# A graph network on one Trainium2 core: adjacency for 38 destination tiles, the other 11 tiles' first sums from gathered rows

## The chip, the cores and the metric

The kernel runs on one core of a Trainium2 chip. The metric is the time of one execution on the device in microseconds; lower is better. A profiled execution gives the trace from which all rows below are read. Engines: TensorE (PE, its weight loads PEld), VectorE (DVE), ScalarE (ACT), GpSimd (POOL), SyncE (SP, which only issues DMAs here). Each runs its own instructions in order and waits on semaphores for the others.

## What is computed

6250 nodes with 128 features, 100,000 directed edges sorted by destination. Four layers follow, each on the layer-normed, rectified state and added to it. The change touches only the first sum of layer 0 and what is made for it:

```python
h = jnp.maximum(_layernorm(x, axis=-1), 0.0)
# layer 0
msgs = x[src]
agg_sum = jax.ops.segment_sum(msgs, dst, num_segments=N)
cnt = jax.ops.segment_sum(jnp.ones((src.shape[0],)), dst, num_segments=N)
aggs = agg_sum / jnp.maximum(cnt, 1.0)[:, None]
out = jnp.concatenate([x, aggs], axis=1) @ W_fuse.T + b_fuse + alpha * x_spectral
# then batch norm, gelu; layer 1: relations, layer 2: attention and feed-forward
# layer 3: ten times
agg = jax.ops.segment_sum(norm[:, None] * xk[src], dst, num_segments=n)
xk = (1.0 - ALPHA) * agg + ALPHA * h
```

## The kernel before

**Tiles.** Nodes are cut into NT = 49 tiles of 128. Edges stand 128 to a column; column (or edge tile) k holds edges 128k and on, and since they are sorted it touches the destinations near 8k. `near(k)` lists its destination tiles, one or two of them; `near_last[m]` is the last column that touches tile m.

**The adjacency.** For each destination tile i the kernel builds the columns of a count matrix, source node by destination node, as fp8: BK = 26 blocks of BD = 5 destinations each. Keys of up to 128 edges of each block are gathered early by GpSimd (L881), decoded by VectorE (L2338 to L2345), counted (L2347) and turned by TensorE into `slot_c`, one column a block. All this holds NB blocks in BS columns of 128.

**The build loop** runs over i and over 13 pairs q of blocks. For a block VectorE writes two one-hots, of the source within its tile (L2365, 128 wide) and of source tile and destination (L2367, 245 wide), into a ring of HOT = 6. TensorE multiplies them (L1597). ScalarE copies a pair out of PSUM into `made`, a ring of MADE = 4 tiles (L1200). When a tile's 13 pairs are out, SyncE stores it to `adj` in DRAM (L688).

**Layer 0's sums** ride along: during tile i TensorE multiplies tile i-1's `made` by the node states y16, four of 49 products behind each pair (L1608, one behind the last). y16 holds the states as two f16 halves and a column of ones for the count. ScalarE copies the second half and the count out (L1190) at q = 3 of tile i+1, and VectorE adds both into C (L2356, L2357) before block k = 6 of it. Since the queues are in order, block 6 stands behind ScalarE's pairs 0 to 2.

**After the loop** the counts of captured edges are compared with the number of edges; the kernel takes its dense branch if all are there. **The last layer** already treats the tiles in two ways: for DENSE = 38 of them it loads `adj` again in each of ten steps; for the last POOLED = 11 it gathers the source rows of their edge tiles (L859), writes one-hots of the destinations on VectorE (L2277) and multiplies on TensorE (L1567). So the adjacency of tiles 38 to 48 is read by nothing but layer 0's sums.

## Time and profile before

| what | us |
|---|---|
| median of three runs | 5482.05 |
| the three runs | 5483.43, 5469.74, 5482.05 |
| profiled execution | 5473.77 |
| its span, first to last instruction | 5471.9 |

The page of the profile gives busy time by engine: TensorE 4486.4 us (82% of the span), VectorE 3022.5 (55%), ScalarE 1054.3, GpSimd 3214.8. These are means over stages with different limits. The stages: loads and preparation to 130 us, the build loop to 666, the rest of layer 0 to about 784, relations, attention, feed-forward, and from about 3040 the ten steps, in which TensorE is full. What the change is worth is read in the stage it touches.

### The profile page before, as it was taken

How to read it: one execution, taken by the hardware profiler on the slowest of the kernel's cores; microseconds unless marked ns; L12 is line 12 of the kernel's file. 1: busy time of each engine (PE TensorE's matmuls, PEld its weight loads, DVE VectorE, ACT ScalarE, POOL GpSimd, SP SyncE). 2: the span in 40 equal slices, each digit the busy share in tenths (PEclk: the TensorE clock that was granted, in tenths of full speed). 3: DMA queues.
4: the chain of work that ended last, by engine and by line, in shares of the span. 5: the costliest groups of instructions: out<-in, count | busy, mean ns of one | idle time of the engine just before them, and what ended most of it. 6: DMA issues, size and time to landing. Idle time of an engine off the chain costs nothing. (4 is left out here: it accounts for less than half of the span.)

```text
span 5471.9 us, 97167 instructions
## 1 busy us (share of the span) xinstructions
PE 4486.4 (82%) x33994; PEld 3739.4 (68%) x33994; DVE 3022.5 (55%) x9610; ACT 1054.3 (19%) x2965; POOL 3214.8 (59%) x3380
## 2 busy tenths in 40 slices
PE   1888849999999265566667799999999999999997
PEld 1555526666666265555555688888888888888886
DVE  5888845555555467777775543343434344343444
ACT  2888731111111201111115100000000000000000
POOL 1000027777776277777760567676767767676775
PEclk9999979999999567766778899999999999999999
DMA  3111122222222243434330566666666666665665
GB/s 121 75 75 72 76 64 67 66 67 66 67 67 57 63 97 97 94 96 98 95 85 36 159 193 187 189 196 184 199 188 194 187 185 201 185 197 184 196 190 181
DMA packets 353802, 696.74 MB, mean 127 GB/s; under 512 B 98849, under 2 KB 233287, under 8 KB 353024
## 3 DMA queue, kind: packets, MB, share of 16 engines
q1 hardware_dynamic: 245648, 466.34, 26.9%
q0 software_dynamic: 107648, 223.88, 16.0%
q8 instruction: 290, 4.75, 0.4%
q14 instruction: 216, 1.77, 0.1%
HBM read 596.34 MB, written 93.92 MB: 126 GB/s over the span
## 5 line engine op out<-in xcount | busy, mean ns | idle before, releaser
L809 POOL DMA_INDIRECT arena<-table,src_i x782 | 741.2, 948 | 904.7 <-DMA table<-A 666.6
L859 POOL DMA_INDIRECT arena<-table,src_i x890 | 846.0, 951 | 529.1 <-DMA table<-E 254.7
L859 POOL DMA_INDIRECT arena<-x_spill,src_i x890 | 847.2, 952 | 352.0 <-issue 252.4
L824 POOL DMA_INDIRECT E<-gat_table,src_i x782 | 755.6, 966 | 337.8 <-issue 234.4
L1364 PE MATMUL ps<-E,arena 128*128 128x288 f32 (+7 forms) x3116 | 790.8, 406 | 90.2 <-DMA arena<-table,src_i 88.1
L1549 PE MATMUL ps<-E,arena 128*128 128x256 f16 x6370 | 726.6, 275 | 58.8 <-DVEq L2268 46.4
L1549 PE MATMUL ps<-A,arena 128*128 128x256 f16 x6370 | 725.4, 275 | 0.6 <-issue 0.2
L1549 PEld LDWEIGHTS ps<-E,arena 128*128 128x128 fp8e4 x6370 | 627.6, 99 | 138.5 <-issue 60.8
L1364 PEld LDWEIGHTS ps<-E,arena 128*128 128x128 f32 x3116 | 507.6, 194 | 309.5 <-issue 145.1
L1549 PEld LDWEIGHTS ps<-A,arena 128*128 128x128 fp8e4 x6370 | 627.5, 99 | 78.9 <-issue 1.9
L2294 DVE SCALAR_TENSOR_TENSOR O<-ps,sc_b,O 128x128 f32<-128x128 f32 x260 | 91.2, 351 | 825.6 <-PE ps L1549 747.7
L1416 PE MATMUL ps<-arena,B 128*128 128x144 f32 x2332 | 530.8, 384 | 2.3 <-DVE arena L2026 2.3
L1929 DVE SCALAR_TENSOR_TENSOR E<-arena,pt 128x512 f32<-128x512 bf16 x782 | 527.5, 742 | 3.0 <-PE ps L1364 2.9
L1416 PEld LDWEIGHTS ps<-arena,B 128*128 128x128 f32 x2332 | 435.6, 257 | 2.5 <-issue 2.5
L1200 ACT ACTIVATE E<-ps 128x490 fp8e4<-128x490 f32 (+1 forms) x637 | 378.3, 595 | 101.6 <-PE ps L1597 84.9
L1427 PE MATMUL pt<-ident,E 128*128 128x128 f32 x56 | 26.0, 464 | 436.1 <-ACT E L1031 436.1
L1608 PE MATMUL pt<-arena,E 128*128 128x258 f16 x2401 | 371.8, 274 | 0.9 <-ACT E L1200 0.9
L2367 DVE TENSOR_SCALAR O<-arena 128x245 bf16<-128x245 bf16 x1274 | 365.8, 287 | 0.0
L1597 PE MATMUL ps<-O 128*128 128x245 bf16 x1274 | 279.1, 274 | 70.3 <-DVE O L2367 67.1
L1549 PE MATMUL pt<-E,arena 128*128 128x256 f16 x2940 | 330.8, 273 | 0.1
L1549 PE MATMUL pt<-A,arena 128*128 128x256 f16 x2940 | 330.7, 273 | 0.0
L2365 DVE TENSOR_SCALAR O<-arena 128x128 bf16<-128x128 bf16 x1274 | 320.4, 252 | 0.5 <-PE ps L1597 0.4
(325 smaller groups left out, 5549.5 us busy)
## 6 DMA issues: line engine op xcount, KB each, us to landing
arena<-adj SPq DMA_DIRECT2D x386, 784.0 KB
adj<-E SPq DMA_DIRECT2D x49, 784.0 KB, 3.3
arena<-table,src_i POOLq DMA_INDIRECT x1672
O<-dst_rows SPq DMA_DIRECT2D x112, 224.0 KB, 3.4
x_spill<-A SPq DMA_DIRECT2D x245, 64.0 KB
table<-E SPq DMA_DIRECT2D x245, 64.0 KB
arena<-x_spill,src_i POOLq DMA_INDIRECT x890
E<-gat_table,src_i POOLq DMA_INDIRECT x782, 3.3
```

The costliest lines, as they stand in the source:

```text
L809: pool.indirect_dma_start(out=rows_ring[:, k % RING, :], out_offset=None, in_=table, in_offset=bass.IndirectOffsetOnAxis(ap=src_i[:, k:k + ...
L824: pool.indirect_dma_start(out=att_rows[:, b % 3 * AB + at, :], out_offset=None, in_=gat_table, in_offset=bass.IndirectOffsetOnAxis(ap=src_ ...
L859: pool.indirect_dma_start(out=y_rows[:, g % ERING, k, :], out_offset=None, in_=(table, x_spill)[half], in_offset=bass.IndirectOffsetOnAxis ...
L1200: act.activation(made[:, i % MADE, :, 2 * BD * q:2 * BD * q + w], ps[pair % 4][:, 0:w * NT].rearrange("p (d j) -> p j d", j=NT), ACT.Copy, ...
L1364: mm = pe.matmul(ps[m % 4][:, (lo - WD * m) * BASES:(hi - WD * m) * BASES], rows_ring[:, k % RING, :], m_ring[:, k % MS, lo - first_dst(k) ...
L1416: mm = pe.matmul(ps[i % 2][:, 0:WL2], edge_hot[:, (2 * b + half) % 3, k % AH, i % 2 * P:(i % 2 + 1) * P], weighted_rows[:, b % 2, k, :], s ...
L1549: mm = pe.matmul(bank_of(x)[:, 0:2 * D], adj_ring[:, u, i * P:(i + 1) * P], y[:, i, :], start=(p == 0), stop=(p == NT - 1))
L1597: pe.matmul(ps[pair % 4][:, h * BW:(h + 1) * BW], hot_src[:, g % HOT, :], hot_code[:, g % HOT, 0:BW], start=True, stop=True).then_inc(sem( ...
L1608: mm = pe.matmul(pt[0][:, m % 2 * 512:m % 2 * 512 + 2 * LO], made[:, m % MADE, j, :], y16[:, j, :], start=(j == 0), stop=(j == NT - 1))
L1929: dve.scalar_tensor_tensor(m_ring[:, k % MS, :, :], bc(iota_h[:, 0:WD], BASES), dst_rel[:, k:k + 1], row_bc(made_c[:, c % 2, at, :], WD), ...
L2365: dve.tensor_scalar(hot_src[:, g % HOT, :], iota_h, slot_c[:, g // P, 0, g % P:g % P + 1], None, ALU.is_equal)
L2367: dve.tensor_scalar(hot_code[:, g % HOT, 0:BW], iota_w[:, 0:BW], slot_c[:, g // P, 1, g % P:g % P + 1], None, ALU.is_equal).then_inc(sem(" ...
```

## The change

The build loop, `adj`, `slot_c` and the keys go over DENSE = 38 tiles. For the other 11, layer 0's sums are made beside the loop:

- SyncE writes y16 to a new table `first_rows` (129 words a row) and the states to `table`, before the adjacency stores. `table` was written later and only in the other branch.
- GpSimd gathers 178 columns of source rows, in groups of EG0 = 16 into a ring of 32 rows that lies in A.
- VectorE writes a 256-wide f16 one-hot of the destination for each column (L2436 after the change), in groups of four, before block k = 16 of tiles 4 to 37.
- TensorE multiplies them (L1648) behind the last pair of tiles 4 to 37, about five columns a tile, 258 products in all.
- When a tile of the eleven is complete, ScalarE copies it out at q = 4 of the next tile and VectorE takes it over before k = 8. Ten are completed in tiles 8 to 36, the last in tile 37.
- The check of captured edges counts the edges of the eleven tiles too.

```diff
-NB = NT * BK
+NB = DENSE * BK
+EG0, HOT_BASE, USED_BASE = 16, 2, 3
...
+        first_rows = dram("first_rows", (NP, LO))
...
+        junk = E[:, 5120:5120 + ET]
+        dst_near = arena[:, 12096:12096 + ET - 600]
+        rows0 = A[:, 0:2 * EG0 * LO].rearrange("p (s f) -> p s f", f=LO)
+        hot0 = A[:, 2 * EG0 * LO:2 * EG0 * LO + EHOT * EG * P].bitcast(F16).rearrange("p (g k d) -> p g k d", g=EHOT, k=EG)
...
+        taken, edges_in, done0, done_in = 0, {}, [], {}
+        for i in range(DENSE + 1):
+            upto = max(0, min(EDGE_TILES, EDGE_TILES * (i - 3) // (DENSE - 4)))
+            edges_in[i] = range(taken, upto)
+            taken = max(taken, upto)
+            done0 += [i - 1] if i else []
+            done_in[i] = [m for x in edges_in[i] for m in range(DENSE, NT) if near_last[m] == edge_first + x]
+            done0 += done_in[i]
+        place0 = {m: p for p, m in enumerate(done0)}
+        hots_in = {i: [x // EG for x in edges_in[i] if x % EG == 0] for i in edges_in}
...
+            sp.wait_ge(sem("hT"), PTN)
+            sp.wait_ge(sem("y_lower"), PTN)
+            sp.dma_start(first_rows.rearrange("(t p) f -> p t f", p=P),
+                         arena[:, 0:NT * LO].rearrange("p (t f) -> p t f", f=LO)).then_inc(sem("table0"), 16)
+            sp.dma_start(table_v, nodes(A)).then_inc(sem("table0"), 16)
+
             adj_v = adj.rearrange("(j p) b -> p j b", p=P)
-            for i in range(NT):
+            for i in range(DENSE):
                 sp.wait_ge(sem("blocks_out"), (i + 1) * (BK // 2))
                 sp.dma_start(adj_v[:, i, 0:NP], made_u8[:, i % MADE, :]).then_inc(sem(f"adj_stored{i % MADE}"), 16)
             for k in range(MADE):
-                sp.wait_ge(sem(f"adj_stored{k}"), 16 * ((NT + MADE - 1 - k) // MADE))
+                sp.wait_ge(sem(f"adj_stored{k}"), 16 * ((DENSE + MADE - 1 - k) // MADE))
             sp.wait_ge(sem("judged"), 1)
             dense = sp.value_load(verdict[0:1, 0:1], min_val=0, max_val=1)
             with sp.If(dense == 1):
...
+            pool.wait_ge(sem("table0"), 32)
+            pool.wait_ge(sem("decoded"), 1)
+            for x in range(EDGE_TILES):
+                g = x // EG0
+                if g >= 2 and x % EG0 == 0:
+                    pool.wait_ge(sem("edge_used0"), USED_BASE + (g - 1) * (EG0 // EG))
+                pool.indirect_dma_start(
+                    out=rows0[:, x % (2 * EG0), :], out_offset=None, in_=first_rows,
+                    in_offset=bass.IndirectOffsetOnAxis(ap=src_i[:, edge_first + x:edge_first + x + 1], axis=0)
+                ).then_inc(sem(f"edge_rows{g % 2}"), 16)
             pool.wait_ge(sem("judged"), 1)
...
-            for i in range(NT + 1):
+            def sums_out(m):
+                p = place0[m]
+                act.wait_ge(sem("multiplied0"), p + 1)
+                if p >= 2:
+                    act.wait_ge(sem("agg0"), p - 1)
+                act.activation(lower_sum[:, p % 2, :], bank0_of(m)[:, D:2 * LO - 1], ACT.Copy).then_inc(sem("counted"), 1)
+
+            for i in range(DENSE + 1):
                 for q in range(BK // 2):
-                    if q == 3 and i >= 2 or i == NT and q == 6:
-                        m = i - 2 if q == 3 else i - 1
-                        act.wait_ge(sem("multiplied0"), m + 1)
-                        if m >= 2:
-                            act.wait_ge(sem("agg0"), m - 1)
-                        act.activation(lower_sum[:, m % 2, :], pt[0][:, m % 2 * 512 + D:m % 2 * 512 + 2 * LO - 1],
-                                       ACT.Copy).then_inc(sem("counted"), 1)
-                    if i == NT:
+                    if q == 3 and i >= 2:
+                        sums_out(i - 2)
+                    if q == 4 and i >= 1:
+                        for m in done_in[i - 1]:
+                            sums_out(m)
+                    if q == 6 and i == DENSE:
+                        sums_out(i - 1)
+                        for m in done_in[i]:
+                            sums_out(m)
+                    if i == DENSE:
...
-            for i in range(NT + 1):
+            def bank0_free(m):
+                if m >= 2 and m - 2 < DENSE and m < DENSE or m - 2 >= DENSE:
+                    pe.wait_ge(sem("agg0"), place0[m - 2] + 1)
+                    pe.wait_ge(sem("counted"), place0[m - 2] + 1)
+
+            def edge_products(x):
+                g, k, tile = x // EG, x % EG, edge_first + x
+                if x % EG0 == 0:
+                    r = x // EG0
+                    pe.wait_ge(sem(f"edge_rows{r % 2}"), 16 * BS + 16 * sum(
+                        min(EG0, EDGE_TILES - q * EG0) for q in range(r % 2, r + 1, 2)))
+                if k == 0:
+                    pe.wait_ge(sem("edge_hot0"), HOT_BASE + g + 1)
+                for m in (m for m in near(tile) if m >= DENSE):
+                    first = max(near_first[m], edge_first)
+                    if tile == first:
+                        bank0_free(m)
+                    mm = pe.matmul(bank0_of(m)[:, 0:2 * LO], hot0[:, g % EHOT, k, m % 2 * P:(m % 2 + 1) * P],
+                                   rows0[:, x % (2 * EG0), :].bitcast(F16), start=(tile == first), stop=(tile == near_last[m]))
+                    if tile == near_last[m]:
+                        mm.then_inc(sem("multiplied0"), 1)
+                if k == EG - 1 and tile < TILES - 1:
+                    mm.then_inc(sem("edge_used0"), 1)
+
+            for i in range(DENSE + 1):
                 for q in range(BK // 2):
-                    if i < NT:
+                    if i < DENSE:
                         pair = i * (BK // 2) + q
                         if pair >= 4:
                             pe.wait_ge(sem("blocks_out"), pair - 3)
...
+                for x in edges_in[i]:
+                    edge_products(x)
             pe.wait_ge(sem("facts"), 1)
             pe.matmul(ps[0][0:1, 0:2], ones[:, 0:1], facts[:, :], start=True, stop=True).then_inc(sem("facts_ps"), 1)
...
+            link(dve.tensor_scalar(Bi[:, ET:2 * ET - edge_first], Bi[:, edge_first:ET], 2 * P - 1, None, ALU.bitwise_and))
+            link(dve.tensor_copy(dst_near[:, 0:ET - edge_first], Bi[:, ET:2 * ET - edge_first]))
...
+            link(dve.scalar_tensor_tensor(limit[:, :], block_n[:, :], float(NB), limit[:, :], ALU.is_lt, MUL))
...
-            for i in range(NT + 1):
+            link(dve.scalar_tensor_tensor(junk, dst_f[:, 0:ET], float(DENSE * P), ones[:, 0:1].to_broadcast([P, ET]),
+                                          ALU.is_ge, MUL, accum_out=below[:, 0:1]))
+
+            def sums_kept(m):
+                p = place0[m]
+                dve.wait_ge(sem("multiplied0"), p + 1)
+                dve.wait_ge(sem("counted"), p + 1)
+                dve.tensor_scalar(cnt[:, m:m + 1], lower_sum[:, p % 2, 0:1], 1.0 / UNIT, None, MUL)
+                dve.tensor_tensor(nodes(C)[:, m, :], bank0_of(m)[:, 0:D], lower_sum[:, p % 2, 1:LO], ADD
+                                  ).then_inc(sem("agg0"), 1)
+
+            def edge_hots(g):
+                if g >= EHOT:
+                    dve.wait_ge(sem("edge_used0"), USED_BASE + g - EHOT + 1)
+                for k in range(group_size(g)):
+                    x = g * EG + k
+                    a = dve.tensor_scalar(hot0[:, g % EHOT, k, :], iota_w, dst_near[:, x:x + 1], UNIT, ALU.is_equal, MUL)
+                a.then_inc(sem("edge_hot0"), 1)
+
+            for i in range(DENSE + 1):
                 for k in range(BK):
-                    if i >= 2 and k == 6 or i == NT and k == 8:
-                        m = i - 2 if k == 6 else i - 1
-                        dve.wait_ge(sem("multiplied0"), m + 1)
-                        dve.wait_ge(sem("counted"), m + 1)
-                        dve.tensor_scalar(cnt[:, m:m + 1], lower_sum[:, m % 2, 0:1], 1.0 / UNIT, None, MUL)
-                        dve.tensor_tensor(nodes(C)[:, m, :], pt[0][:, m % 2 * 512:m % 2 * 512 + D],
-                                          lower_sum[:, m % 2, 1:LO], ADD).then_inc(sem("agg0"), 1)
-                    if i < NT:
+                    if i >= 2 and k == 6:
+                        sums_kept(i - 2)
+                    if i >= 1 and k == 8:
+                        for m in done_in[i - 1]:
+                            sums_kept(m)
+                    if i == DENSE and k == 12:
+                        sums_kept(i - 1)
+                        for m in done_in[i]:
+                            sums_kept(m)
+                    if k == 16:
+                        if hots_in[i] and hots_in[i][0] == 0:
```

The order of the engines, at three places. TensorE at the end of tile i = 5 and the start of the next, before: the last pair, one sum product, the next tile's first pair, and the sums of tile 5.

```order
L1597 MATMUL ps<-O 128x245 [waits hot,blocks_out]
L1597 MATMUL ps<-O 128x245 [waits hot]
L1608 MATMUL pt<-arena,E 128x258
L1597 MATMUL ps<-O 128x245 [waits hot,blocks_out]
L1597 MATMUL ps<-O 128x245 [waits hot]
L1608 MATMUL pt<-arena,E 128x258 [waits agg0,counted,y_lower,blocks_out]
L1608 MATMUL pt<-arena,E 128x258 x3
```

And now (L1664 is L1597, L1673 is L1608 before):

```order
L1664 MATMUL ps<-O 128x245 [waits hot,blocks_out]
L1664 MATMUL ps<-O 128x245 [waits hot]
L1673 MATMUL pt<-arena,E 128x258
L1648 MATMUL pt<-A 128x258 x3
L1648 MATMUL pt<-A 128x258 [waits filter]
L1648 MATMUL pt<-A 128x258
L1664 MATMUL ps<-O 128x245 [waits hot,blocks_out]
L1664 MATMUL ps<-O 128x245 [waits hot]
L1673 MATMUL pt<-arena,E 128x258 [waits agg0,counted,y_lower,blocks_out]
L1673 MATMUL pt<-arena,E 128x258 x3
```

Five products of gathered rows (L1648, with a wait for the one-hots under the name `filter`) stand between the last sum product and the next tile's first pair.

VectorE in tile i = 9, around blocks 5 to 8, before:

```order
L2365 TENSOR_SCALAR O<-arena 128x128 [waits built]
L2367 TENSOR_SCALAR O<-arena 128x245
L2356 TENSOR_SCALAR cnt<-arena 128x1 [waits counted,multiplied0]
L2357 TENSOR_TENSOR C<-pt,arena 128x128
L2365 TENSOR_SCALAR O<-arena 128x128 [waits built]
L2367 TENSOR_SCALAR O<-arena 128x245
L2365 TENSOR_SCALAR O<-arena 128x128 [waits built]
L2367 TENSOR_SCALAR O<-arena 128x245
L2365 TENSOR_SCALAR O<-arena 128x128 [waits built]
```

And now (L2461 and L2463 are the one-hots, L2427 and L2428 the taking over):

```order
L2461 TENSOR_SCALAR O<-arena 128x128 [waits built]
L2463 TENSOR_SCALAR O<-arena 128x245
L2427 TENSOR_SCALAR cnt<-arena 128x1 [waits counted,multiplied0]
L2428 TENSOR_TENSOR C<-pt,arena 128x128
L2461 TENSOR_SCALAR O<-arena 128x128 [waits built]
L2463 TENSOR_SCALAR O<-arena 128x245
L2461 TENSOR_SCALAR O<-arena 128x128 [waits built]
L2463 TENSOR_SCALAR O<-arena 128x245
L2427 TENSOR_SCALAR cnt<-arena 128x1 [waits counted,multiplied0]
L2428 TENSOR_TENSOR C<-pt,arena 128x128
L2461 TENSOR_SCALAR O<-arena 128x128 [waits built]
```

A second taking over, of tile 38, has come two blocks behind the first. The same happens in the tile behind each of the other nine. Further on in tile 9, where there was only the row of one-hots, there is now a group of four L2436 (shared semaphore `filter_ps`: their ring slot is free):

```order
L2461 TENSOR_SCALAR O<-arena 128x128 [waits built]
L2463 TENSOR_SCALAR O<-arena 128x245
L2461 TENSOR_SCALAR O<-arena 128x128 [waits built]
L2463 TENSOR_SCALAR O<-arena 128x245
L2436 TENSOR_SCALAR A<-arena 128x256 [waits filter_ps]
L2436 TENSOR_SCALAR A<-arena 128x256 x3
L2461 TENSOR_SCALAR O<-arena 128x128 [waits built]
L2463 TENSOR_SCALAR O<-arena 128x245
```

The four stand between the one-hots of block 15 and those of block 16; some tiles have eight.

GpSimd from the key gathers on, before:

```order
L881 DMA arena<-key_pad,starts_i 128x128 [waits starts_found,keys_stored]
L881 DMA arena<-key_pad,starts_i 128x128 x9
L885 TENSOR_LOAD verdict [waits judged]
L885 ISA x2
L886 COMPARE_AND_BRANCH
```

And now:

```order
L906 DMA arena<-key_pad,starts_i 128x128 [waits starts_found,keys_stored]
L906 DMA arena<-key_pad,starts_i 128x128 x7
L915 DMA A<-first_rows,src_i 128x129 [waits decoded,table0]
L915 DMA A<-first_rows,src_i 128x129 x31
L915 DMA A<-first_rows,src_i 128x129 [waits filter_ps]
L915 DMA A<-first_rows,src_i 128x129 x15
L915 DMA A<-first_rows,src_i 128x129 [waits filter_ps]
```

There are two key gathers fewer, and the row gathers stand between them and the verdict, which waits for the end of the loop: 32 at once, then 16 for each 16 columns that TensorE has used.

## Rows read from the trace of the kernel before

**Rows 1.** Lines: duration ns min/median/max, first and last start us

```profile
L2365 DVE TENSOR_SCALAR O<-arena x1274: 240/251/270, 129.8 to 666.0; 128x128 bf16<-128x128 bf16 x182
...
L2367 DVE TENSOR_SCALAR O<-arena x1274: 274/286/305, 130.0 to 666.1; 128x245 bf16<-128x245 bf16 x182
```

**Rows 2.** Busy us of each engine in a stretch of the build

```profile
core 0: us, PE busy (x) PEld busy (x) DVE busy (x) ACT busy (x) POOL busy (x), PEclk, DMA share, GB/s
200.00:400.00 200.00, 173.21 (x1369) 116.25 (x1367) 175.24 (x985) 161.54 (x492) 0.00 (x0) 1.00 0.18 74
```

**Rows 3.** Timeline: start us, us, engine, line, op, [idle before]; one turn

```profile
303.91 0.27 PE L1608 MATMUL pt<-arena,E 128*128 128x258 f16 x1
...
304.75 0.62 PE L1608 MATMUL pt<-arena,E 128*128 128x258 f16 x4
...
305.58 0.29 DVE L2367 TENSOR_SCALAR O<-arena 128x245 bf16<-128x245 bf16 x1
...
306.28 0.58 ACT L1200 ACTIVATE E<-ps 128x490 fp8e4<-128x490 f32 x1
...
306.85 0.27 ACT L1190 ACTIVATE arena<-pt 128x129 f32<-128x129 f32 x1
307.22 0.15 DVE L2356 TENSOR_SCALAR cnt<-arena 128x1 f32<-128x1 f32 x1 [1.35 <-ACT arena L1190]
...
307.49 0.25 DVE L2365 TENSOR_SCALAR O<-arena 128x128 bf16<-128x128 bf16 x1
...
307.84 0.25 DVE L2365 TENSOR_SCALAR O<-arena 128x128 bf16<-128x128 bf16 x1
308.00 0.28 DVE L2367 TENSOR_SCALAR O<-arena 128x245 bf16<-128x245 bf16 x1
```

**Rows 4.** Line of taking over a sum; its timeline row near the end

```profile
L2356 DVE TENSOR_SCALAR cnt<-arena x49: 153/154/155, 153.3 to 673.5; 128x1 f32<-128x1 f32 x49
...
658.94 0.15 DVE L2356 TENSOR_SCALAR cnt<-arena 128x1 f32<-128x1 f32 x1 [1.35 <-ACT arena L1190]
```

**Rows 5.** Timeline of VectorE ahead of the build

```profile
46.68 1.03 DVE L1790 SCALAR_TENSOR_TENSOR E<-E,first_v,arena 128x782 f32<-128x782 int32 x1
...
97.71 0.35 DVE L2324 SCALAR_TENSOR_TENSOR E<-E,first_v,arena 128x128 f32<-128x128 int32 x1 [19.01 <-ACT A L956]
...
107.16 7.11 DVE L2335 SCALAR_TENSOR_TENSOR arena<-A,arena 128x896 f16<-128x896 f32 x7 [4.68 <-ACT arena L1178]
...
119.20 0.83 DVE L2338 TENSOR_SCALAR E<-arena 128x1280 int32<-128x1280 int32 x1 [4.93 <-DMA arena<-key_pad,starts_i]
```

**Rows 6.** The line of the key gathers on GpSimd

```profile
L881 POOL DMA_INDIRECT arena<-key_pad,starts_i x10: 944/946/1702, 102.8 to 116.6; - x10
```

**Rows 7.** Timeline, edge one-hots and a gather in the step stage

```profile
3092.70 0.99 DVE L2277 TENSOR_SCALAR weight_e<-w_gat,dst_f 128x256 f16<-128x256 bf16 x4
...
3095.18 1.65 DVE L2277 TENSOR_SCALAR rows<-w_gat,dst_f 128x256 f16<-128x256 bf16 x8
3095.19 0.95 POOL L859 DMA_INDIRECT arena<-table,src_i  x1 [0.30 <-issue]
```

**Rows 8.** Timeline of TensorE, edge products in the step stage

```profile
3326.01 1.25 PE L1567 MATMUL pt<-arena,rows 128*128 128x256 f16 x10
```

**Rows 9.** DMA issues: KB each, median us to landing

```profile
table<-A SPq DMA_DIRECT2D x1, 3136.0 KB, 13.3
```

**Rows 10.** Timeline of TensorE, relation stage, after two pauses

```profile
898.53 1.99 PE L1364 MATMUL ps<-E,arena 128*128 128x224 f32 x8 [2.13 <-DMA arena<-table,src_i]
...
918.52 3.62 PE L1364 MATMUL ps<-E,arena 128*128 128x224 f32 x8 [2.05 <-DMA arena<-table,src_i]
```

**Rows 11.** Timeline, relation stage: a long VectorE operation and a gather

```profile
792.33 2.03 DVE L1954 TENSOR_SCALAR C<-C 112x3584 f32<-112x3584 f32 x1
792.41 2.76 POOL L809 DMA_INDIRECT arena<-table,src_i  x1 [0.30 <-issue]
```

**Rows 12.** Busy us in a stretch of the attention stage, clock behind them

```profile
2000.00:2100.00 100.00, 56.29 (x385) 52.69 (x384) 66.82 (x127) 9.00 (x42) 75.66 (x80) 0.74 0.39 97
```

More of the change, by code:

```diff
@@ L338, in build, with bank0_of @@
         edge_banks = [pt[1][:, 0:512], pt[1][:, 512:1024]]
+        def bank0_of(i):
+            return (pt[0][:, i % 2 * 512:i % 2 * 512 + 512] if i < DENSE else edge_banks[i % 2])
         def bank_of(i):
@@ L1195, in _ @@
                         act.wait_ge(sem(f"adj_stored{i % MADE}"), 16 * (i // MADE))
[L1196 removed]
+                        act.wait_ge(sem("multiplied0"), place0[i - MADE] + 1)
                     w = min(2 * BD, P - 2 * BD * q)
@@ new lines, in _ @@
+            for i in range(DENSE + 1):
+                for k in range(BK):
+                    if i >= 2 and k == 6:
[9 more added lines that the diff above has]
+                        if hots_in[i] and hots_in[i][0] == 0:
+                            dve.wait_ge(sem("table0"), 32)
+                        for g in hots_in[i]:
+                            edge_hots(g)
+                    if i < DENSE:
@@ L2385, in _ @@
             for k in range(MADE):
-                dve.wait_ge(sem(f"adj_stored{k}"), 16 * ((NT + MADE - 1 - k) // MADE))
+                dve.wait_ge(sem(f"adj_stored{k}"), 16 * ((DENSE + MADE - 1 - k) // MADE))
             dve.sem_inc(sem("judged"), 1)
```

20 lines of the change are left out of this document (8 added, 12 removed).

## The prediction

> **What bounds the kernel now.** I first cut the span into stretches and looked at which engine is full in each. The layers from 784 us on are not touched by the change, so the only stretch to read closely is the one that builds the adjacency: the first block operand is written at 129.8 us, the last at 666.1 [rows 1], 536 us for 49 destination tiles. In the middle of it TensorE 173, VectorE 175 and ScalarE 162 us of 200 are busy [rows 2]; none is full, so I went to the timeline of one turn from a tile to the next.
>
> The turn shows a chain [rows 3]. VectorE makes two one-hots (L2365, L2367) for each block, TensorE multiplies them, ScalarE copies a pair of blocks out, and TensorE puts four products of the sums of the tile before (L1608) behind each pair. While VectorE runs free it starts a block every 0.356 us (307.49, 307.84). TensorE is quicker than that and waits for the one-hots. But once a tile VectorE stands before block 6: it has to take over the sums of an older tile (L2356, L2357), and ScalarE copies these out (L1190) only behind its third pair of the new tile. The last one-hot starts at 305.58, the copy of its pair at 306.28, L1190 at 306.85, L2356 at 307.22 after 1.35 us idle, and block 6 at 307.49. So a tile is 26 x 0.356 = 9.26 us of VectorE's pace and 1.7 us of this stall. The rows agree: 46 turns from 153.3 to 658.94 make **10.99 us a tile** [rows 4]. Whatever is put on VectorE is on the path; whatever is put on TensorE at the end of a tile is on it through the stall.
>
> **What goes.** Eleven of 49 tiles: 11 x 10.99 = **-120.9 us**. Their share of the sums (11 x 49 products) and their copies lie inside that period and are not counted again.
>
> **What goes ahead of it.** 38 x 26 blocks need 8 columns of block keys where 49 x 26 needed 10. Two of the ten counts on VectorE at 97.7 us (0.35 and a read-out, some 0.40 with it) are dropped [rows 5]: -0.8. Two of ten key gathers, 0.95 us each and 0.30 between them [rows 6]: -2.5. The decoding and counting from 119.20 to 129.8 shrinks by a fifth: -2.1. One new count over 784 columns costs what a 782-column one does [rows 5], 1.03 and the read-out: +1.1. Sum **-4.3 us**. The counts at 46.68 shrink too, and two small operations join them, but VectorE waits for the zeroed tables later, so they are free. Against it: the SyncE queue now writes two tables of 3.1 MB as soon as L2335 is done (114.3 in this trace [rows 5]), just where the last key gathers land; I take the delay as nothing and keep 3 us for the range.
>
> **One-hots for the edge sums, on VectorE.** 178 operations of 128x256, f16 from bf16. The same form is in the trace at L2277: eight in 1.65 us, each about 0.30 long, so (1.65 - 0.30) / 7 = 0.195 apart [rows 7]. They stand between blocks 15 and 16 of tiles 4 to 37, where VectorE is the pacer: 178 x 0.195 = **+34.7 us**. Nothing hides them.
>
> **Products of the edge rows, on TensorE.** 258 matmuls of 128x258, 5 to 12 behind each tile. The like of it, L1567, runs ten in 1.25 us: (1.25 - 0.27) / 9 = 0.109 apart [rows 8]. They stand behind the last sum product (303.91 in [rows 3]) and ahead of the next tile's first pair. Today the first sum product there waits for ScalarE until 304.75. With n products the next pair starts at 304.02 + 0.109 n and the sums two products later, so the stall chain is late by 0.109 n - 0.52, which is nothing for n = 5 and 0.79 for n = 12. Over the 33 turns (252 products) that is 10 us; with some hand-over I take **+13**. Ends: 0 if the chain had more slack than I see, 28 (all 258 in full).
>
> **Sums of the eleven tiles.** Each is one more L1190 and one more L2356/L2357, and the order puts them one pair behind the present stall: ScalarE takes them out behind pair 3, VectorE wants them before block 8. So VectorE writes blocks 6 and 7 and stands again. By [rows 3] block 7's second one-hot starts at 308.00; from such a start to the next free block was 305.58 to 307.49, 1.91 us, where 0.20 is normal: 1.7 each. Ten fall inside the build: **+17 us**. The eleventh lies in the tail. Ends 10 and 22.
>
> **Gathers.** GpSimd does nothing in the build [rows 2]; now it issues 178 gathers, the first behind both table writes. A write of this size took 13.3 us [rows 9], so it starts near 114.5 + 2 x 13.3 = 141, and 16 rows are there by 163; TensorE first asks at the end of tile 4, near 180. From then on 34 tiles of about 12.4 us use 178 rows, 16 in 38 us, while 16 gathers at 1.25 take 20. The first adjacency store stands in the same queue behind the tables and is due only at tile 4. So the gathers are covered, and cost only what they take from VectorE. A gather that lay wholly under eight L2277 kept its 0.95, and they kept their pace; four L2277 that began with a gather at 3092.70 took 0.99 where 0.30 + 3 x 0.195 = 0.88 is normal [rows 7]. So 0 to 0.11 a gather; most meet no such start there, but the builder never pauses: **+4 us**, ends 0 and 20.
>
> **Clock.** In the build the granted clock is 1.00 [rows 2]. At a finished tile two TensorE pauses of 1.2 to 1.8 us now stand 1 us apart. In the relation stage a pause of 2.05 us was followed by a stretch at the lower clock: eight products that took 1.99 us took 3.62 [rows 10]. At 1.6 us each for two of ten: **+3**, ends 0 and 16. **Tail**: the last products and one more small addition, +0.7.
>
> **Sum.** -120.9 - 4.3 + 34.7 + 13 + 17 + 4 + 3 + 0.7 = -52.8. A tile with edge work becomes about 10.99 + 1.02 + 0.4 + 0.1 = 12.5 us. Against the profiled execution, 5473.8 us (span 5471.9), that is 5421; against the median of the runs, 5482.05, it is 5429. Two of three runs stood at the upper figure, so I forecast **5428 us**.
>
> **Rival 1, slower: the gathers set the pace.** VectorE's builder never leaves a gap. At 792.33 a VectorE operation of 2.03 us was running when a gather began, and that gather took 2.76 us; another in the key gathers took 1.70 [rows 6, 11]. If the chain of short one-hots held every gather as that long operation did, each would take 2.76 + 0.30 = 3.06 us, 178 of them 545, the last rows would be there at 141 + 545 + 3 = 689 instead of the last one-hot at 613, and with the unchanged tail of 7 us the stage would end at 696, 22 later than today: **5504 us** on the median. It decides from about 2.4 us a gather (38 us for 16). Against it: the gather at 3095.19 [rows 7], short operations that do not add up. The Trainium skill, page "SBUF — State Buffer", section "Who interferes with whom", says that a VectorE operation in a two-port mode holds the port pair shared with GpSimd for its whole length and the other blocks; the section "SBUF: two separate sides" of that page puts such a DMA at 3100 ns where it takes 620 alone. Worked out from that figure (an estimate), 178 x 3.4 = 605 us would end the stage some 80 us later than today. The row at 792 agrees with a wait for the end of one operation; the row at 3095.19 speaks against one that lasts over many short ones. I give both readings 6 in 100.
>
> **Rival 2, the added work piles up.** Products in full (28), gathers cost VectorE 0.11 each (20), the clock falls at each finished tile (16), stalls of 2.2 (22): -120.9 - 1.3 + 34.7 + 28 + 22 + 20 + 16 + 0.7 = -0.8, **5481 us**, no change. Each end has a row, but all together only with bad luck: 6 in 100.
>
> **Rival 3, the clock stays low.** In the attention stage TensorE was busy 56 in 100 us and the clock was 0.74 [rows 12]. At the lower level the 75 products of a tile, 7.9 us now, need 15.8, and a tile is 17 us: 38 x 17 = 646, 110 more than today's 536. TensorE would still be busy some 8 of 12.5 us, near today's share, so 2 in 100.
>
> **Rival 4, more gain.** If the products and the second stall fit into the slack: -120.9 - 4.3 + 34.7 + 0 + 10 + 0 + 0 + 0.7 = -80, 5402 us. 8 in 100; it lies at the edge of the range.
>
> **How the numbers follow.** Forecast 78 in 100, rivals 6, 6, 2 and 8. The range takes in rival 4 and about two thirds of the way to the bad ends of the unknown terms: **5400 to 5458**. A measurement here tells 0.3% (16 us) from no change; below 5466 is faster: forecast, rival 4 and nothing else, 0.86. Within 0.3%: rival 2, 0.06. Slower: rivals 1 and 3, 0.08.
>
> **What would show it.** First one-hot near 125.5; the period of a tile without finished sums near 12.5 and with them 14.2; the last one-hot near 613; gathers at 0.95 to 1.2 us with GpSimd idle between groups of 16; TensorE's clock 1.00 through the stage; the relation and later stages of equal length. It is wrong if VectorE idles before L2436 or TensorE for a gather, if gathers pass 2.4 us, or if the stages behind the build change their length.

## The result and the profile after

The changed kernel takes **5424.68 us** in the median of four runs (5410.16 to 5427.68), against 5475.9 for the kernel before in the same series (5464.22 to 5483.43). The ratio is 0.9904 [0.9884, 0.9925]: 51 us faster. The forecast was 5428, range 5400 to 5458. The profiled execution took 5427.68 us, its span 5425.9, which is 46.0 less than the 5471.9 of before.

**The build.** First I read the lines that answer to [rows 1] and [rows 4]. The columns are the duration in ns (min/median/max) and the first and last start; under them stands who waited for the line.

```profile
L2461 DVE TENSOR_SCALAR O<-arena x988: 232/244/438, 133.0 to 617.5; 128x128 bf16<-128x128 bf16 x198
...
L2427 DVE TENSOR_SCALAR cnt<-arena x49: 153/154/154, 156.7 to 625.1; 128x1 f32<-128x1 f32 x49
...
L1222 ACT ACTIVATE arena<-pt x49: 271/272/280, 156.3 to 624.7; 128x129 f32<-128x129 f32 x49
...
who waited for it (us, times):
  DVE cnt L2427: 81.2, 48
```

The build starts at 133.0 us instead of 129.8 and ends at 617.5 instead of 666.0: 484.6 us long where it was 536.1 (from the unrounded starts). From L2461 (L2365 before) I took the time from each tile's first block to the next one's. Of tiles 4 to 36, the 24 with edge work and one taking over average 12.43 us, the nine with two of them 14.48. Before it was 10.99 for all [rows 4].

**A turn.** The same view as [rows 3], at a tile with ten edge products and a finished sum.

```profile
236.90 0.27 PE L1673 MATMUL pt<-arena,E 128*128 128x258 f16 x1
237.01 1.27 PE L1648 MATMUL pt<-A 128*128 128x258 f16 x10
238.12 0.37 PE L1664 MATMUL ps<-O 128*128 128x245 bf16 x2
238.33 0.61 PE L1673 MATMUL pt<-arena,E 128*128 128x258 f16 x4
...
240.41 0.27 ACT L1222 ACTIVATE arena<-pt 128x129 f32<-128x129 f32 x1
240.79 0.15 DVE L2427 TENSOR_SCALAR cnt<-arena 128x1 f32<-128x1 f32 x1 [2.01 <-ACT arena L1222]
241.64 0.55 PE L1664 MATMUL ps<-O 128*128 128x245 bf16 x2 [1.39 <-DVE O L2463]
...
242.79 0.27 ACT L1222 ACTIVATE arena<-pt 128x129 f32<-128x129 f32 x1
243.17 0.15 DVE L2427 TENSOR_SCALAR cnt<-arena 128x1 f32<-128x1 f32 x1 [1.32 <-ACT arena L1222]
244.03 0.74 PE L1664 MATMUL ps<-O 128*128 128x245 bf16 x2 [1.39 <-DVE O L2463]
244.56 1.07 PE L1673 MATMUL pt<-arena,E 128*128 128x258 f16 x4
```

Three things are to be seen. The ten products take 1.27 us on TensorE and push the next pair, and so the ScalarE copy of the older sum, back: VectorE stands 2.01 us where it stood 1.35. Two blocks later it stands again, 1.32, for the finished tile. And behind the second pause TensorE runs slow: four products take 1.07 us where they took 0.61 some 6 us earlier.

**The clock.** Busy time of each engine in three stretches, the first the one of [rows 2], the last behind the two pauses shown above; the figure behind the counts is the granted clock (1.00 is the 2.4 GHz level, 0.50 the 1.2 GHz level).

```profile
core 0: us, PE busy (x) PEld busy (x) DVE busy (x) ACT busy (x) POOL busy (x), PEclk, DMA share, GB/s
200.00:400.00 200.00, 162.04 (x1269) 116.72 (x1269) 165.67 (x910) 134.07 (x418) 73.33 (x77) 0.96 0.28 89
400.00:600.00 200.00, 161.49 (x1273) 115.98 (x1272) 167.49 (x921) 135.58 (x421) 67.81 (x70) 0.97 0.27 87
...
243.25:250.00 6.75, 5.97 (x28) 4.14 (x29) 6.37 (x36) 2.85 (x9) 0.95 (x1) 0.50 0.10 22
```

The clock is no longer 1.00: between 200 us and the last one-hot it stands at the lower level in six stretches, 31 us in all. Before there was none. All six begin within the second pause of a finished tile or 0.4 us behind it; at four of the ten finished tiles the clock stays at 1.00.

**The gathers.** The lines of the one-hots and of the gathers for the edge sums:

```profile
L2436 DVE TENSOR_SCALAR A<-arena x178: 267/276/428, 182.8 to 614.1; 128x256 f16<-128x256 bf16 x178
...
L915 POOL DMA_INDIRECT A<-first_rows,src_i x178: 941/948/1061, 144.5 to 582.0; - x178
its engine sat idle before it (us, times) until:
  PE pt L1648: 215.7, 10
```

A gather takes 0.948 us, never above 1.061, and GpSimd spends 215.7 us waiting for free ring slots. Beside VectorE's one-hots a gather is as quick as the one in [rows 7].

**Ahead of the build.** The timeline from the last key gather on:

```profile
114.41 1.70 POOL L906 DMA_INDIRECT arena<-key_pad,starts_i  x1 [0.30 <-issue]
...
115.38 0.38 SPq L707 DMA_DIRECT2D first_rows<-arena  x1
115.81 13.01 SPq L709 DMA_DIRECT2D table<-A  x1
123.29 0.69 DVE L2408 TENSOR_SCALAR E<-arena 128x1024 int32<-128x1024 int32 x1 [7.99 <-DMA arena<-key_pad,starts_i]
```

The last of eight key gathers begins at 114.41, earlier than the last of ten before (116.6 in [rows 6]), but VectorE gets the keys at 123.29, later than the 119.20 of [rows 5]. Its rest to the first block is shorter as forecast, 9.7 us for 10.6. The two table writes land more slowly than the 13.3 us of [rows 9]. The view is of 110 to 150 us alone, since the same name is written again later; columns are KB and us from issue to landing.

```profile
first_rows<-arena SPq DMA_DIRECT2D x1, 3160.5 KB, 20.7
table<-A SPq DMA_DIRECT2D x1, 3136.0 KB, 28.4
```

The second was issued 0.4 us behind the first, so both have landed 28.9 us after the first's issue, at 144.3.

**The balance** of the two spans: start of the build +3.1, the build -51.5, all behind its last one-hot +2.4, together -46.0.

### The profile page after: what moved, and what is told of

Its sections match the earlier page's. It is cut to its first block and busy times, and to the rows that moved or that the text cites. A ratio compares the mean times of both kernels' runs of the same rounds, so it can differ in the third digit from the quotient of the medians.

```text
span 5425.9 us, 95336 instructions
## 1 busy us (share of the span) xinstructions
PE 4412.7 (81%) x33423; PEld 3704.8 (68%) x33423; DVE 2955.5 (54%) x9208; ACT 955.1 (18%) x2677; POOL 3390.4 (62%) x3554
## 5 line engine op out<-in xcount | busy, mean ns | idle before, releaser
L1470 PE MATMUL pt<-ident,E 128*128 128x128 f32 x56 | 26.6, 475 | 440.9 <-ACT E L1065 440.9
L915 POOL DMA_INDIRECT A<-first_rows,src_i x178 | 171.6, 964 | 295.3 <-PE pt L1648 215.7
L1243 ACT ACTIVATE E<-ps 128x490 fp8e4<-128x490 f32 (+1 forms) x494 | 293.4, 594 | 150.6 <-PE ps L1664 141.5
L1592 PEld LDWEIGHTS pt<-E,arena 128*128 128x128 fp8e4 x2940 | 287.5, 98 | 33.8 <-issue 0.5
L1592 PEld LDWEIGHTS pt<-A,arena 128*128 128x128 fp8e4 x2940 | 287.7, 98 | 33.3
```

What stands on the lines that cost most here:

```text
L915: pool.indirect_dma_start(out=rows0[:, x % (2 * EG0), :], out_offset=None, in_=first_rows, in_offset=bass.IndirectOffsetOnAxis(ap=src_i[:, ...
L1243: act.activation(made[:, i % MADE, :, 2 * BD * q:2 * BD * q + w], ps[pair % 4][:, 0:w * NT].rearrange("p (d j) -> p j d", j=NT), ACT.Copy, ...
L1592: mm = pe.matmul(bank_of(x)[:, 0:2 * D], adj_ring[:, u, i * P:(i + 1) * P], y[:, i, :], start=(p == 0), stop=(p == NT - 1))
```

## The experiments

Theory A: the sum of the prediction is right term by term, VectorE's order and its once-a-tile wait decide, and the gathers cost almost nothing. Theory B: the gathers and VectorE slow each other. Theory C: the terms overlap or the later stages give something back, so that single edits do not add up. Each run below moves or removes one term. All edits but one are to the changed kernel.

The table has, for each profile, the first one-hot, the length of the build (first to last one-hot), the mean time from the start of the block before to the start of block 6, 8 and 16 in tile 4 and all later ones (0.36 where nothing stands between), and the time at the lower clock in the build from 150 us on. The last column is from the granted clock, all others are worked out from the starts of the one-hot lines in the traces.

```
                 start   build   at 6   at 8   at 16   low clock
before           129.8   536.1   2.09   0.36   0.36     0
after            133.0   484.6   2.45   0.86   1.39    31
again            131.3   485.3   2.45   0.86   1.39    34
hots_at_6        125.9   452.1   2.53   0.86   0.37    24
products_at_3    125.9   472.8   2.11   0.85   1.41    10
finished_at_3    133.0   467.5   2.48   0.36   1.39     3
tables_later     124.8   482.2   2.40   0.85   1.40    31
all_four         125.8   421.8   2.21   0.36   0.36     0
all_four_again   125.9   421.6   2.21   0.37   0.36     0
no_edge_sums     128.2   415.2   2.10   0.36   0.36     3
gathers_doubled  125.1   525.7   3.56   0.85   1.40    65
before_at_12     130.8   466.7   0.36   0.36   0.36     0
all_four_at_12   126.6   406.7   1.40   0.36   0.37     3
```

### The change unedited, once more

> The changed kernel itself, unedited, as the mark for the runs beside it. Both theories: 0.9904 of the kernel before, build loop (first to last one-hot of the blocks) 484.6 us as in its first trace, first one-hot near 133 us if the late key gathers are a property of the kernel and not of one run.

Median 5429.54 us (5426.83 to 5431.25), ratio 0.9908 [0.9893, 0.9923]. Build and gaps repeat within 1 us and 0.01 us. What single edits do to the build can be read from the traces, then; the start wanders by 1.7 us (131.3, not 133).

### The edge one-hots before block 6

```diff
                 for k in range(BK):
+                    if k == 6:
+                        if hots_in[i] and hots_in[i][0] == 0:
+                            dve.wait_ge(sem("table0"), 32)
+                        for g in hots_in[i]:
+                            edge_hots(g)
                     if i >= 2 and k == 6:
                         sums_kept(i - 2)
...
-                    if k == 16:
-                        if hots_in[i] and hots_in[i][0] == 0:
-                            dve.wait_ge(sem("table0"), 32)
-                        for g in hots_in[i]:
-                            edge_hots(g)
```

> Only the place of the edge one-hots on VectorE is changed: from before block 16 to before block 6, ahead of the taking over of the sums, where VectorE idles 73 us over 45 waits. Theory A (a chain: at block 6 VectorE waits for TensorE and ScalarE whatever it does, elsewhere it is the pacer): 0.78 or 1.58 us of one-hots a tile fit into an idle time of about 1.6 us, so the build loop loses 33 us, to 452. Theory B (VectorE is simply full, the order of its work does not matter): 0. Theory C (TensorE and ScalarE need the pause at block 16 to catch up): 10 to 18 us.

5385.63 us (5382.24 to 5399.38), ratio 0.9839 [0.9826, 0.9853]. The same 178 operations stand where VectorE waits for the older sum. The gap at 16 is gone, the one at 6 grows from 2.45 to 2.53 only, and the build is 32.5 us shorter. VectorE's wait at the taking over is less by about the same amount, 47.9 us for 81.2:

```profile
L2427 DVE TENSOR_SCALAR cnt<-arena x49: 141/154/155, 149.3 to 585.5; 128x1 f32<-128x1 f32 x49
its engine sat idle before it (us, times) until:
  ACT arena L1222: 47.9, 43
```

So at block 16 the one-hots had cost their full price, as the sum said, and at block 6 they cost next to nothing. This is theory A; it is also the largest gain of any single edit.

### The edge products behind pair 3 of the next tile

```diff
                 for q in range(BK // 2):
+                    if q == 3 and i >= 1:
+                        for x in edges_in[i - 1]:
+                            edge_products(x)
                     if i < DENSE:
...
-                for x in edges_in[i]:
-                    edge_products(x)
```

> Only the place of the edge products on TensorE is changed: from behind the last pair of a tile to before pair 3 of the next, where TensorE waits 1.3 to 1.6 us for VectorE. Theory A: the sums of the next tile start at once again, the gap before block 6 falls from 2.45 to 2.06 us on the mean, 33 times 0.4: 13 us less, build loop 472. Theory B (TensorE's total is what counts): 0. Finished tiles come later by the products, so up to 3 us may be given back at block 8.

5407.72 us (5404.6 to 5410.2), ratio 0.9869 [0.9854, 0.9885]. The build is 11.8 us shorter and the gap at 6 is back at 2.11, next to the 2.09 of before. The products' place at the end of a tile had cost 12 us; behind the ScalarE copy for which VectorE waits they cost nothing that is seen. They also fill one of the two pauses of a finished tile, and the lower clock falls from 31 us to 10. Three low stretches are left, though, and each comes with a pause that stands alone (1.39 or 1.47 us).

### Finished tiles taken over beside the dense one

```diff
                         sums_out(i - 2)
-                    if q == 4 and i >= 1:
                         for m in done_in[i - 1]:
                             sums_out(m)
...
                         sums_kept(i - 2)
-                    if i >= 1 and k == 8:
                         for m in done_in[i - 1]:
                             sums_kept(m)
```

> A finished tile of the eleven is taken out and over right behind the dense tile at pair 3 and block 6, not one pair later. Theory A (the second stall is the chain of a pair through TensorE and ScalarE, paid again because two one-hots stand between): the ten gaps before block 8 (2.0 us each) go back to 0.36, and each costs some 0.6 us more before block 6: 10 to 13 us less, build loop 472 to 475. Theory B (the cost is the extra copy and addition themselves, or the bank that has to be free): 0 to 3 us less.

5409.25 us (5396.19 to 5413.22), ratio 0.9863 [0.9848, 0.9878]. The build is 17.1 us shorter, more than theory A's 10 to 13: the gap at 8 is 0.36 again, but the one at 6 grows only from 2.45 to 2.48, 1 us over the whole build where theory A allowed 0.6 at each of ten. One wait serves both sums. The lower clock falls from 31 us to 3; the stretch that is left comes behind a single pause of 1.73 us.

### The table writes behind the landing of the keys

```diff
             sp.wait_ge(sem("y_lower"), PTN)
+            sp.wait_ge(sem("keys_in"), 16 * BS)
             sp.dma_start(first_rows.rearrange("(t p) f -> p t f", p=P),
```

> The two table writes on the SyncE queue wait for the landing of the key gathers; nothing else is changed. Theory A (6.3 MB of writes delay the last key gathers, which landed 7.2 us after their issue where they took 1.6 before): the first one-hot of the blocks comes 5 to 6 us earlier, near 127.5, and the whole time falls by as much; the row gathers begin some 5 us later and stay covered. Theory B (the late landing was chance): 0.

5419.67 us (5414.58 to 5424.34), ratio 0.989 [0.9875, 0.9905], beside 0.9908 for the unedited kernel: the two intervals overlap, so the total does not settle it. The trace does for the start: 124.8 instead of 133.0, even earlier than the 127.5 of theory A. The decoding waits 0.36 us for the keys in place of 7.99:

```profile
115.10 0.69 DVE L2409 TENSOR_SCALAR E<-arena 128x1024 int32<-128x1024 int32 x1 [0.36 <-DMA arena<-key_pad,starts_i]
...
115.16 0.38 SPq L708 DMA_DIRECT2D first_rows<-arena  x1
```

The same gain comes without the edit in some runs of the others. In the one-hot run the write stood behind the last key gather by chance:

```profile
113.02 1.70 POOL L906 DMA_INDIRECT arena<-key_pad,starts_i  x1 [0.30 <-issue]
...
116.00 0.38 SPq L707 DMA_DIRECT2D first_rows<-arena  x1
116.22 0.69 DVE L2408 TENSOR_SCALAR E<-arena 128x1024 int32<-128x1024 int32 x1 [0.30 <-DMA arena<-key_pad,starts_i]
```

There the decoding starts 1.5 us after the gather's issue has ended (114.72 to 116.22). In the changed kernel the write is issued at 115.38, while the last gather (114.41 to 116.11) is still being issued, and the decoding starts 7.2 us after its end (6.8 in the repeat). Three traces have the write inside the last gather and the long wait (the change twice, and the one with the finished tiles moved: write 115.44, gather 114.47 to 116.17, decoding at 123.35). In four the write came behind the gather's issue (by 0.27 us at least, with the products moved: write 114.85, decoding 116.20), and the decoding stood at 115.46 to 116.85, again 1.5 to 1.7 us after the gather's end. It is a race of two queues: a write 0.7 us ahead of that end costs 5.6 us, one 0.3 us behind it nothing.

### The edge work left out

```diff
-            for x in range(EDGE_TILES):
+            for x in range(0):
...
-                for x in edges_in[i]:
-                    edge_products(x)
...
+            link(dve.memset(nodes(C)[:, DENSE:NT, :], 0.0))
+            link(dve.memset(cnt[:, DENSE:NT], 16.0))
...
-                    if k == 16:
-                        if hots_in[i] and hots_in[i][0] == 0:
-                            dve.wait_ge(sem("table0"), 32)
-                        for g in hots_in[i]:
-                            edge_hots(g)
```

This kernel leaves out the gathers, one-hots, products and taking over of the eleven tiles; their first sums are zero. Both table writes stay. Clearing the sums takes VectorE 1.7 us ahead of the build.

> Left out: the row gathers, the edge one-hots, the edge products and the taking over of the eleven tiles (their sums are set to zero and their counts to 16); the two table writes stay. It shows what the edge work costs as the changed kernel places it. Theory A: 34.7 + 13 + 17 and 2 or 3 for the clock, 65 to 70 us less, build loop 38 tiles at 10.99 less the short first ones, near 416. If gathers slowed VectorE as well, up to 20 us more than that.

5349.24 us (5345.21 to 5354.25), ratio 0.9766 [0.9752, 0.9779]. The build takes 415.2 us, 120.9 less than before, exactly 11 tiles at 10.99. All edge work in the build costs 484.6 - 415.2 = 69.4 us; the terms of the prediction for it were 34.7 + 13 + 17 + 4 + 3 = 71.7.

### Every gather issued twice

```diff
                 ).then_inc(sem(f"edge_rows{g % 2}"), 16)
+                pool.indirect_dma_start(
+                    out=again[:, x % (2 * EG0), :], out_offset=None, in_=first_rows,
+                    in_offset=bass.IndirectOffsetOnAxis(ap=src_i[:, edge_first + x:edge_first + x + 1], axis=0)
+                ).then_inc(sem(f"edge_rows{g % 2}"), 16)
...
-                    pe.wait_ge(sem(f"edge_rows{r % 2}"), 16 * BS + 16 * sum(
+                    pe.wait_ge(sem(f"edge_rows{r % 2}"), 16 * BS + 32 * sum(
```

The second gather fetches the first 8 words of the same rows into a spare place.

> Every row gather is followed by a second one of the same rows, 8 words of each, into unused memory: the work of GpSimd is doubled, 2.5 us a column, and the start of gathers beside VectorE too. Theory A (the gathers decide from about 2.4 us a column): 16 columns take 40 us and 3 to land, TensorE uses them up in 38.7, so TensorE waits about 4 us at each of nine groups: 20 to 40 us slower than the changed kernel. Theory B (each start of a gather costs VectorE 0.1 us): 18 us more on top, spread over the tiles. Theory C (the threshold lies well above 2.5 us): 0 to 4 us.

5453.01 us (5450.04 to 5463.24), ratio 0.9957 [0.9943, 0.997]: some 24 us slower than the unedited change, the build 41.1 us longer (its start was one of the early ones). Who waits is in the lines (columns as above; the third fence has count, then busy us and mean ns, then idle before and releasers):

```profile
L1653 PE MATMUL pt<-A x258: 271/273/422, 189.8 to 652.1; 128*128 128x258 f16 x129
its engine sat idle before it (us, times) until:
  DMA arena<-first_rows,src_i: 55.7, 14
```

That view adds up the matrix products and their weight loads, which wait side by side. The view of the second gather, L920, tells them apart:

```profile
who waited for it (us, times):
  PEld pt L1653: 28.8, 7
  PE pt L1653: 26.8, 7
```

```profile
L920 POOL DMA_INDIRECT arena<-first_rows,src_i x178 | 171.9, 966 | 54.6 <-issue 54.6
L916 POOL DMA_INDIRECT A<-first_rows,src_i x178 | 171.7, 965 | 101.7 <-issue 52.4 <-DMA table<-A 34.6 <-PE pt L1653 14.7
```

So TensorE now waits for rows seven times, 28.8 us in all, about the 4 us a time that theory A gave; GpSimd waits 14.7 us for slots where it waited 215.7. Of the 41.1 us of the build 38 are in the gap at 6. A column costs 2 x (0.965 + 0.30) = 2.53 us of GpSimd, just past the 2.4 at which rival 1 was to decide. But the other half of rival 1 and of theory B falls: with twice the gathers, each still takes 0.965 us. Free blocks of VectorE cost 8.06 us a tile against 7.96 (22 of the 26 steps, those to 0, 6, 8 and 16 left out), though TensorE stood at the lower clock for 65 us of this build, so 0.10 is the most that the extra gathers took in these steps.

### All four edits

The one-hots before block 6, the products behind pair 3, the table writes behind the keys, and finished tiles at the wait of the dense tile, one tile later than above, since their products now end in the next tile.

> Edge one-hots before block 6, edge products before pair 3 of the next tile, a finished tile taken out and over ahead of the dense one two tiles later, table writes behind the key gathers. Theory A: the gains add up (33 + 13 + 12 + 5.5) as far as the idle time before block 6 reaches: 55 to 65 us less than the changed kernel, 5360 to 5370 us, build loop near 425 to 430. Theory B: no gain but the last 5 us.

5358.7 us (5355.17 to 5360.06), ratio 0.978 [0.9767, 0.9794]. The three edits in the build gave 32.5, 11.8 and 17.1 us alone, together 61.4; the build is 62.8 shorter. They add up, against theory C. Of 69.4 us of edge work 6.6 are left (421.8 against 415.2); by the medians it is 9.5 us. The same kernel later:

> all_four itself, unedited, beside the two others: 0.978 of the kernel before, build loop 422 us.

5358.48 us (5355.75 to 5362.3), ratio 0.9786 [0.9773, 0.98].

### The wait itself, in the kernel before

The gaps say that VectorE stands 1.7 us a tile for a copy that ScalarE has in its queue behind three pairs. If so, asking six blocks later should remove the wait. The edit is to the kernel before, and moves only VectorE's side:

```diff
-                    if i >= 2 and k == 6 or i == NT and k == 8:
-                        m = i - 2 if k == 6 else i - 1
+                    if i >= 2 and k == 12 or i == NT and k == 14:
+                        m = i - 2 if k == 12 else i - 1
```

> The kernel before with one number changed: VectorE takes a tile's sums over before block 12, not before block 6 (in the last turn 14, not 8). Theory A (the 1.35 us idle time and the rest of the 1.7 us stall are VectorE waiting for ScalarE's third pair; six blocks later the copy is long out): the tile becomes 26 x 0.356 + 0.27 = 9.5 to 9.7 us, 46 turns: 60 to 68 us less than before, 5412 to 5420 us. Theory B (TensorE or ScalarE need the pause once a tile: 13 pairs at their own pace are 8.6 us and the turn 0.5, near VectorE's 9.3): the wait only moves, 0 to 20 us.

5409.77 us (5402.59 to 5414.62), ratio 0.9877 [0.9862, 0.9892]: 67 us, more than the whole change brought. The build takes 466.7 us in place of 536.1, and VectorE and TensorE, at 175 and 173 of 200 in [rows 2], are full:

```profile
200.00:400.00 200.00, 198.73 (x1577) 134.14 (x1575) 200.00 (x1135) 183.73 (x568) 0.00 (x0) 1.00 0.21 86
```

```profile
L2356 DVE TENSOR_SCALAR cnt<-arena x49: 132/133/155, 154.3 to 605.0; 128x1 f32<-128x1 f32 x49
its engine sat idle before it (us, times) until:
  ACT arena L1190: 6.7, 2
```

The wait was pure waiting: no resource was short, only the place in the order was early.

### All four, and the taking over at block 12

> The kernel all_four with the taking over before block 12 as well; the edge one-hots stay before block 6, where there is now no idle time that hides them. Theory A: a tile is 9.6 + 1.0 of one-hots and 0 to 0.4 of products, 10.6 to 11.0 us where all_four has 11.1 on the mean: 4 to 18 us less than all_four, 5341 to 5355 us. Theory B (the stall was needed): no less than all_four, or 10 us more.

```diff
-                    if i >= 2 and k == 6:
+                    if i >= 2 and k == 12:
                         for m in done_in[i - 2]:
                             sums_kept(m)
                         sums_kept(i - 2)
-                    if i == DENSE and k == 12:
+                    if i == DENSE and k == 14:
```

**5339.56 us** (5334.87 to 5345.81), ratio 0.9754 [0.974, 0.9767], the fastest of all, 137 us under the kernel before. VectorE is busy for 200 of 200 us:

```profile
200.00:400.00 200.00, 193.83 (x1534) 133.90 (x1532) 200.00 (x1110) 164.19 (x506) 94.90 (x96) 1.00 0.34 109
```

Its build of 406.7 us is 38 x 9.26 = 352 for the blocks, 35 for the edge one-hots, 49 x 0.27 = 13 for the taking over, and some 7 more. A gather takes 0.970 us in the median here, 1.400 at most: even beside a VectorE that never stops, gathers are not held for long. Against the kernel before with the same late taking over, the medians differ by 5409.77 - 5339.56 = 70 us, but the build by 60.0 only: eleven tiles of 9.26 us, less the 35 us of one-hots, which nothing hides any more, and the 7. The other 10 lie outside it: 4.2 ahead of the build, the rest behind it, where the traces differ by up to 15.6 us and no run has an edit.

## Why the prediction was right

**Eleven tiles, -120.9.** Right to the tenth: 415.2 us against 536.1 without the edge work.

**One-hots, +34.7.** The gap at 16 is 1.39 on average instead of 0.36: 34 tiles x 1.03 = 35.0. Moved into the wait they give back 32.5.

**Products, +13.** The gap at 6 is 2.45 instead of 2.09: 34 x 0.36 = 12.2, and 11.8 when moved. The working from the turn, "late by 0.109 n - 0.52", held: with ten products the wait was 2.01 instead of 1.35, 0.66 more where it says 0.57.

**Second stall, +17.** The mean gap at 8 is 0.86 instead of 0.36, over 34 tiles 17.0; 17.1 when moved.

**Gathers on VectorE and clock, +4 and +3.** The free steps of a tile cost 7.96 us instead of 7.83: 38 x 0.13 = 4.9 for both, 2 less than forecast. With all four edits, when the clock never fell, it is 7.89: so some 2.3 us for the gathers (and whatever else is in that difference; without any edge work it is 7.85) and 2.6 for the clock. That split is argued, not measured by itself. That the second pause brings most low stretches is shown by the two runs that take a pause away (31 us to 3, and to 10); that it takes two is not: in the runs without double pauses six low stretches came with a single pause, three with the products moved and one each in three others. The size of the clock's term was luck: two falls at 1.6 us each were forecast, six came, and by the 2.6 each cost some 0.4. The line "TensorE's clock 1.00 through the stage" was wrong and stood against the working's own +3.

**The build, then**: forecast -120.9 + 34.7 + 13 + 17 + 4 + 3 = -49.2, measured -51.5.

**What goes ahead, -4.3, was wrong in sign**: +3.1. The step that failed is "I take the delay as nothing and keep 3 us for the range". The place was named, the table writes just where the last key gathers land, but the price was not 0 to 3 us but 5.6 (7.2 against 1.6 before, from the end of the gather's issue to the decoding). Of the other 1.8 us, 1.6 are there long before the keys:

```profile
99.33 0.35 DVE L2394 SCALAR_TENSOR_TENSOR E<-E,first_v,arena 128x128 f32<-128x128 int32 x1 [19.01 <-ACT A L990]
```

The same count began at 97.71 in [rows 5], after the same 19.01 us of waiting. In the other traces with the change's preparation it begins at 97.99 to 99.87, and in the kernel before with the late taking over at 98.86, so this is not shown to be a cost of the change. Where the write missed the gather the build started at 124.8 to 126.6 (128.2 with the 1.7 us of clearing), that is 3.2 to 5.0 us before the 129.8 of before: the -4.3 itself was sound.

**Behind the build**, forecast +0.7, measured +2.4. Over all traces the time behind the last taking over is 4791.5 to 4807.1 us (4798.4 before) and follows no edit, so this is not a cost of the change that I could show. The two writes of the tables took 28.9 us together, not 26.6, and began 0.9 us later than forecast, so the first row gather stood at 144.5 instead of 141; nobody waited for it.

**The rivals.** Rival 1 is out: a gather beside the one-hots is 0.948 us, and the doubled gathers show both that a column of 2.53 us is enough to make TensorE wait and that its cause does not occur. The rule that the prediction named for it did not show itself in this stage. The 1.70 us of the last key gathers beside L2405, seven operations of 1.0 us, fits a gather that is held by a longer VectorE operation; no run moved the one against the other. Rival 2's ends of 28, 22, 20 and 16 were 12, 17, 2 and 3. Rival 3 never came near: the clock was 0.96 and 0.97. Rival 4 was half right in that the work fits into the slack, but only from another place in the order, which the change did not choose.

The range's upper end was not "two thirds of the way" to rival 2: it is 30 of the 53 us, a little over half.

**How much was luck.** The span fell by 46.0 where the sum said 52.8: the start missed by 7.4 and the build by 2.3 the other way, the rest by 1.7. The median of the runs fell by 51. The build carries the result, and its terms were each right to about 2 us, the clock's by luck; the one wrong step, the start, cost 7.4 us in this profile and not in every trace of an edited kernel.

## What to carry to other kernels

When an engine in order waits once a turn for something that another engine has queued behind work of its own, first ask for it later: here six blocks later, one place in the order, brought 67 us, more than a rewrite worth 51. If the wait must stay, put new work into it and not beside it: the same 178 one-hots cost 35 us ten blocks further on and under 3 us ahead of the wait. And a big write that is moved forward on one queue is to be priced against the last small transfer of every other queue that ends at the same time.

## What the runs showed of the hardware

I had not expected that a gather's rows come so late beside a write. From the end of the gather's issue to the decoding it is 1.5 to 1.7 us; it was 6.8 to 7.2 when a write of 3160.5 KB was issued 0.7 us before that end, in three traces of three. With the write held back until the keys were in, VectorE's wait was 0.36 us. Why the write holds the rows up is open. Two such writes, the second issued 0.4 us behind the first, landed 20.7 and 28.4 us after their issues, where one alone took 13.3 in [rows 9].

A pause of 1.39 us of TensorE, one pair and its four products, and another pause of 1.39 us came ahead of a stretch at the lower clock: two one-hot products took 0.74 us where they had taken 0.37 shortly before, four sum products 1.07 where they took 0.61. Two such pauses did not always do it (six of ten finished tiles in the changed kernel, seven of ten in its repeat). One pause a tile, as in the kernel before, was never followed by a low stretch in its build, but in other runs single pauses of 1.39, 1.47, 1.73, 1.74 and 2.04 us were.
